# Sigmoids of the gate loops: kept in PSUM in three steps of four, instead of two

## The reference, cut to what matters

```
hg   = h3 @ Wg[:, :F].T                                  # (8, 32, 768)
qg   = q  @ Wg[:, F:].T + bg                             # (8, 64, 768)
attn = sigmoid(hg[:, :, None, :] + qg[:, None, :, :])    # (8, 32, 64, 768)
qi   = einsum('bnlf,blf->bnf', attn, q)                  # sum over the 64 queries
alpha = sigmoid(h3 @ Wq[:, :F].T + qi @ Wq[:, F:].T + bq)
out  = alpha * tanh(qi) + (1 - alpha) * h3
```

## Time and profile before

| what | value |
|---|---|
| median of 3 runs | 1069.91 us (1068.56 to 1072.1) |
| profiled execution | 1069.65 us |
| its span, first to last instruction | 1067.8 us |
| mean granted TensorE clock | 0.996 of full speed |
| TensorE busy | 1029.7 us, 96% |
| VectorE busy | 767.6 us, 72% |
| ScalarE busy | 574.3 us, 54% |
| GpSimd busy | 263.5 us, 25% |

### The profile page before, as it was taken

The page is one execution under the profiler, slowest core; times in us unless marked ns, Lnnn a source line. Parts: engine busy times, 40 slices in busy tenths (PEclk is TensorE's granted clock), DMA queues, the critical chain, the costliest instruction groups (busy, mean ns, idle before and its releaser), DMA issues.

```text
span 1067.8 us, 17748 instructions
## 1 busy us (share of the span) xinstructions
PE 1029.7 (96%) x7444; PEld 853.1 (80%) x7444; DVE 767.6 (72%) x1106; ACT 574.3 (54%) x612; POOL 263.5 (25%) x166
## 2 busy tenths in 40 slices
PE   8999999999999999999899989999999999999997
PEld 6799986454689984445869879967999999999994
DVE  7993855888754237888654495755989898989873
ACT  0433216888633338888324373424767676767650
POOL 3524704899400027988100000000000000000000
PEclk9999999999999999999999999999999999999999
DMA  8033247221042374221335302614978787878740
GB/s 302 12 126 142 90 144 233 63 66 55 6 178 89 119 231 144 60 60 41 109 129 187 125 1 90 214 49 155 302 254 281 256 279 254 280 256 279 255 168 32
DMA packets 82324, 163.20 MB, mean 153 GB/s; under 512 B 4076, under 2 KB 60168, under 8 KB 81950
## 3 DMA queue, kind: packets, MB, share of 16 engines
q1 hardware_dynamic: 80768, 151.86, 42.0%
q0 software_dynamic: 1472, 10.15, 3.4%
HBM read 158.35 MB, written 0.80 MB: 149 GB/s over the span
## 4 chain that ended last, share of the span: by engine, by line
PE 81%; DVE 11%; issue 3%; ACT 2%; DMA 1%; POOL 0%; SPq 0%; DVEq 0%; ACTq 0%
PE PS L1139 20%; PE PS L803 8%; PE PS L974 7%; PE PS L819 6%; PE PS L602 5%; PE PS L701 5%; PE PS L1122 5%; PE PS L725 4%; PE PS L532 4%; PE PS L621 3%; PE PS L545 3%; PE PS L1155 2%; PE PS L1041 2%; DVE PRD L1756 2%; PE PS L861 2%
## 5 line engine op out<-in xcount | busy, mean ns | idle before, releaser
L2025 DVE TENSOR_TENSOR Wlo<-W,Whi 128x2304 fp32r<-128x2304 f32 x68 | 172.1, 2550 | 18.9 <-ACT Whi L1496 18.9
L1496 ACT CAST Whi<-W 128x2304 fp32r<-128x2304 f32 x68 | 144.4, 2126 | 0.0
L1139 PE MATMUL PS<-Whi,Mhi 128*128 128x384 f32 x408 | 138.1, 338 | 0.0
L1139 PE MATMUL PS<-Wlo,Mhi 128*128 128x384 f32 x408 | 136.6, 335 | 0.0
L1139 PE MATMUL PS<-Whi,Mlo 128*128 128x384 f32 x408 | 136.5, 335 | 0.0
L499 POOL TENSOR_TENSOR PRDP<-arena 128x1024 f32<-128x1024 f32 x48 | 114.7, 2390 | 33.0 <-issue 20.6
L803 PE MATMUL PS<-QH,SEL 128*128 128x512 f32 x384 | 115.8, 422 | 5.9 <-DVE PRD L1756 1.5
L1338 ACT ACTIVATE arena<-PS 128x1024 f32<-128x1024 f32 x96 | 98.5, 1026 | 24.2 <-PE PS L803 24.2
L803 PEld LDWEIGHTS PS<-QH,SEL 128*128 128x128 f32 x384 | 64.8, 188 | 55.8 <-DVE PRD L1756 21.5
L1338 ACT ACTIVATE PS<-PS 128x1024 f32<-128x1024 f32 x96 | 98.0, 1021 | 2.6 <-PE PS L803 2.6
L1139 PEld LDWEIGHTS PS<-Whi,Mhi 128*128 128x128 f32 x408 | 76.9, 188 | 0.4 <-DVE Wlo L2025 0.2
(11 more groups left out here) (306 smaller groups left out, 2421.1 us busy)
## 6 DMA issues: line engine op xcount, KB each, us to landing
W<-in_L_rel SPq DMA_DIRECT2D x68, 1152.0 KB, 6.5
W<-in_W_rel SPq DMA_DIRECT2D x6, 2304.0 KB, 9.2
W<-in_W SPq DMA_DIRECT2D x6, 2304.0 KB, 9.1
arena<-in_qU SPq DMA_DIRECT2D x96, 128.0 KB, 2.7
W<-in_WqT SPq DMA_DIRECT2D x4, 2304.0 KB, 8.7
W<-in_W_root SPq DMA_DIRECT2D x2, 2304.0 KB, 13.3
W<-in_WgT SPq DMA_DIRECT2D x2, 2304.0 KB, 8.5
QH<-QH POOLq DMA_DIRECT2D x2, 1536.0 KB, 9.7
```

Source lines behind the costliest of these rows:

```text
L1139: mm = pe.matmul(PS[:, 4 + s % 2, 0:HALF], MS[a][mb][:, k, j * P:(j + 1) * P], WS[b][w % 3][:, k, :], start=n == 0, stop=n == 17)
L1496: nc.scalar.copy(WS[0][w % 3][:], W[(FIRST34 + r) % 2][:, :, q * HALF:(q + 1) * HALF]).then_inc(w_hi, 1)
L2025: V.tensor_tensor(WS[1][w % 3][:], W[(FIRST34 + r) % 2][:, :, q * HALF:(q + 1) * HALF], WS[0][w % 3][:].bitcast(F32), ALU.subtract).then_i ...
```

## The change: which sigmoids stay in PSUM

`in_psum` now holds for c mod 4 = 0, 1 and 3, all the steps that VectorE multiplies. The buffer `SIGS` goes, and with it ScalarE's wait for the product that read it last. The sigmoid of c mod 4 = 0 is written over its sums in PSUM and VectorE reads it there. Since `sums` asks `in_psum(c - 3)`, the sums of c mod 4 = 3 now wait for VectorE's product of c-3 at L795, where they waited for ScalarE's sigmoid of c-3 at L797. The count of instructions stays the same.

```diff
 def in_psum(n):
 
-    return n % 2 == 1
+    return n % 4 != 2
...
-        SIGS, SIGP = (view(arena, 7936 + 1024 * i, 1024) for i in range(2))
+        SIGP = view(arena, 8960, 1024)
...
                     if in_psum(c):
                         out = sums
-                    elif on_pool(c):
+                    else:
                         out = SIGP
                         if c >= 4:
                             act.wait_ge(pool_prod, by_pool(g * STEPS + c))
-                    else:
-                        out = SIGS
-                        if c >= 4:
-                            act.wait_ge(prod_done, by_dve(g * STEPS + c - 3))
                     nc.scalar.activation(out, sums, ACT.Sigmoid).then_inc(attn_done, 1)
...
-                    sig = PS[:, at_banks(c):at_banks(c) + 2, :].rearrange("p b n -> p (b n)") if in_psum(c) else SIGS
+                    sig = PS[:, at_banks(c):at_banks(c) + 2, :].rearrange("p b n -> p (b n)")
                     V.tensor_tensor(PRD[k % 4], sig, QD[h], ALU.mult).then_inc(prod_done, 1)
```

## The result

The changed kernel takes 1088.15 us (median, 1087.23 to 1088.67), the one before 1070.95 beside it: a ratio of 1.0163, interval 1.0141 to 1.0184. The forecast was 1088, and slower.

A forecast was written before the change was run, and what follows sets the result against it. TensorE was taken as the bound; a new wait for VectorE's product lengthens 21 groups a loop from 4.36 to 4.78 us, 8.9 plus 0.35 at the ends, +18.5 over two loops: 1088 us, range 1079 to 1096.

The forecast's parts named there:

- TensorE is the bound and has no slack: First loop's steady part: TensorE busy 94.05 of 95.4 us, some 1.4 us of slack, so delays are paid at once.
- a ring of 4.78: Sums of 4m, sigmoid, product, sums of 4m+3, reductions, sums of 4m+4: period 4.78 us instead of 4.36 per four-step group.
- The release at 3.11: TensorE may start the sums of 4m+3 3.11 us after those of 4m; without a wait, 2.61; stall 0.50.
- pair A: TensorE's row of four L803 matmuls for steps 4m and 4m+1, followed by reductions of an earlier pair; starts 4.78 apart forecast.
- The ends add 0.35 a loop, nothing outside changes: Loop ends add about 0.35 us to 8.9, making 9.25 a loop; time changing outside the gate loops would refute the forecast.
- SyncE's loads cost nothing: Loads of the next query rows, waiting at L356 and L357, move with the loop; costed at nothing.
- The product in PSUM gives 0.08 a group, 3.7 us by itself: VectorE's product of 4m falls from 1.324 to 1.22 us, ending TensorE's 0.16 wait in every second group.
- pair B: TensorE's L803 matmuls for steps 4m+2 and 4m+3; forecast to split into two and two, waiting for VectorE before the second.
- the new wait was not covered: Rival: product of 4m done before TensorE needs it, groups of 4.28 us, 1066 us, faster; 6%.
- TensorE had no slack to hide it: Rival: the stall only eats TensorE idle time, about 0.4 us in each 4.36; 1069 to 1071 us; 4%.
- the clock stayed at 1.00: Rival: pauses drop TensorE's clock from 2.4 to 1.2 GHz in the loops, near 1257 us; 2%.
- the stall came in every group, not in every second: Rival: the new wait shows only in every second group, +9 us in both loops, 1079 us; 10%.

The follow-up runs named there:

- the order with one reduction between: Changed kernel with TensorE's pair B reordered: sums of 4m+2, one reduction, sums of 4m+3, the other reduction; 1079.77 us, ratio 1.0094 to the kernel before.
- the wait alone: Kernel before with one edit: sums of c = 4m+3 wait for VectorE's product of 4m, no sigmoid moves; 1097.31 us, ratio 1.0254.
- the control with one reduction between: Kernel before, old placement, with TensorE's order sums of 4m+2, one reduction, sums of 4m+3, the other reduction; 1084.74 us, ratio 1.0141.

## Why the prediction was right, step by step

- *TensorE is the bound and has no slack*: right. What was added to its queue came out in the time, 18.3 us in the span (1086.1 against 1067.8), and in the order with one reduction between, TensorE alone set 4.59 a group and the time followed.
- *The wait at L795 closes a ring of 4.78*: right; 4.78 over 21 groups, and the wait alone makes the loss. The release at 3.11 was 3.15 in the group shown, since the product started 0.07 behind its sigmoid there and 0.03 in the group ahead (255.68 + 1.01 to 256.72, which released at 3.09 after its pair A). 1.67 to the next pair A was exact.
- *The ends add 0.35 a loop, nothing outside changes*: the first loop ends at 291.37 against 281.92, 9.45 later (9.25 forecast); of this the 21 groups give 8.88 and the ends 0.57. The second ends at 526.71 against 508.38, 18.33 later, which is the whole difference in the span. So the second loop added 8.9, a little less than the first, because the kernel before lost more in it: its groups took 4.38 there (21 groups from 408.88 to 500.95). No VectorE product in the first loop waits for a DMA, so SyncE's loads cost nothing, as the prediction put them.
- *The product in PSUM gives 0.08 a group, 3.7 us by itself*: mis-sized, and as a term of its own mistaken. It was priced by the old wait. In the ring a longer product counts nearly in full: products of 1.57 and 1.23 in turn, instead of 1.22, made groups of 4.97 instead of 4.78, and the time 9.7 us longer (the wait alone against the change). In another order of TensorE it is worth 5 us, and where VectorE's own order made its products short, GpSimd's got longer, the wait moved to pair B, and no time came. The total was right because the ring was summed with the short product of 1.22 from the start.
- *The rivals*: the new wait was not covered; TensorE had no slack to hide it; the clock stayed at 1.00 in loops with a pause in every 4.8 us; and the stall came in every group, not in every second. The Trainium skill, page "TensorE: Matmul & The Clock Gate", section "A second HAM failure mode: psum-queue depth-cycling", tells of a kernel whose clock swung with short pauses between groups of matmuls that cycle through PSUM banks; no run here shows that.

## What to carry to other kernels

When a buffer is given back later by one engine's instruction, close the loop: add up the links from the first use of the buffer to its next, then what the waiting engine still has to do before the next first use; the sum is the period if it exceeds the busiest engine's work. Check every user of a rotating buffer in the engine's real order, the second of a pair first, for it has the least time, and do it again for each new order. Where a profile names a releaser, look up in the code which count the instruction needs: here the label named a reduction, and the wait was for a sigmoid. And an instruction slowed by contention is priced by who waits for it and for what stands behind it in its queue, not by its own extra time.

## What the runs showed of the hardware

VectorE's product with both operands in the on-chip buffer and GpSimd's work don't share, they take turns. Which of them waits is decided by who starts first: VectorE took 2.55 instead of 1.22 behind a GpSimd product (with 0 and 1 in PSUM), and GpSimd 3.08 on average instead of 2.39 where VectorE started ahead of it (with VectorE's order changed). A row of GpSimd from the kernel before, then a product of each engine with VectorE's order changed, then GpSimd's subtraction in the kernel before (groups by form, 180 to 278 us):

```profile
256.78 2.39 POOL L499 TENSOR_TENSOR PRDP<-arena 128x1024 f32<-128x1024 f32 x1 [0.70 <-issue]
```

```profile
255.52 1.22 DVE L1758 TENSOR_TENSOR PRD<-arena 128x1024 f32<-128x1024 f32 x1
255.84 3.13 POOL L500 TENSOR_TENSOR PRDP<-arena 128x1024 f32<-128x1024 f32 x1 [0.91 <-issue]
```

```profile
L484 POOL TENSOR_TENSOR WR<-W,WH 128x256 fp32r<-128x256 f32 x11 | 19.0, 1724 | 0.0
```

How long the second one takes follows from when the first one ends. VectorE's product ended 1.08 after GpSimd's instruction in each of four runs: at 255.55 against 254.47 with 0 and 1 in PSUM; at 260.25 against 259.17 in the kernel before, where its 1.41 holds a wait for the GpSimd product of 256.78; at 254.44 against 253.36 with the wait alone, and at 257.00 against 255.92 in the control with one reduction between, both behind a subtraction (252.62 + 0.74 and 255.17 + 0.75). GpSimd's product of 255.84 ended 2.23 after VectorE's (258.97 against 256.74). The cost lands on small work too: GpSimd's 128x256 subtraction took 1.72 us on average between such products and 0.73 once VectorE read PSUM.

The Trainium skill, page "SBUF — State Buffer", section "SBUF: two separate sides", calls this an exclusive lock that the first to start holds for the whole instruction. These rows agree.
